# Layer 0's low parts of tiles 4 to 7 as ACT negation plus an adding DMA, ACT's code checks and POOL's bias sums in other places

## The reference

```
# layer 0
e      = leaky_0.2((x * a0) @ x.T)                 # 1024 x 1024, symmetric
alpha  = sigmoid(where(adj == 1, e, -inf))
x1     = layernorm(x + alpha @ x + bias)
# layer 1
H      = x1 @ W ;  s = H @ a_src ;  d = H @ a_dst
E      = where(adj != 0, exp(-leaky_0.2(s_i + d_j)), 0)
out    = layernorm(x1 + elu((E @ H) / rowsum(E)))
```

## Time and profile before

| | |
|---|---|
| median of 3 runs | 1370.85 us (1370.57 to 1371.18) |
| the profiled execution | 1369.6 us |
| its span, first to last instruction | 1367.8 us |
| PE busy | 1275.9 us, 93% |
| DVE, ACT, POOL busy | 1029.2, 856.0, 842.4 us |
| TensorE clock, mean granted | 0.993 |

### The profile page before, as it was taken

The page is one execution under the profiler, slowest core; times in us unless marked ns, Lnnn a source line. Parts: engine busy times, 40 slices in busy tenths (PEclk is TensorE's granted clock), DMA queues, the critical chain, the costliest instruction groups (busy, mean ns, idle before and its releaser), DMA issues.

```text
span 1367.8 us, 27395 instructions
## 1 busy us (share of the span) xinstructions
PE 1275.9 (93%) x7874; PEld 1139.3 (83%) x7874; DVE 1029.2 (75%) x2594; ACT 856.0 (63%) x2130; POOL 842.4 (62%) x1228
## 2 busy tenths in 40 slices
PE   5799999999999999999999999999999998999986
PEld 4788888888888888888888888888888888888875
DVE  5777778787777877778777787877878777787865
ACT  4746757476575756757476575756757567574643
POOL 4746749476583855839466583865839567394732
PEclk9999999999999999999999999999999999999999
DMA  8162350614325162350624415153250623406001
GB/s 173 32 109 74 67 109 19 119 58 87 94 41 102 45 111 73 59 113 12 121 63 73 104 28 110 54 100 80 54 119 16 111 73 65 108 14 124 28 5 34
DMA packets 190352, 101.73 MB, mean 74 GB/s; under 512 B 140656, under 2 KB 173808, under 8 KB 190320
## 3 DMA queue, kind: packets, MB, share of 16 engines
q1 hardware_dynamic: 171888, 67.79, 21.2%
q0 software_dynamic: 18432, 33.56, 14.6%
HBM read 84.55 MB, written 16.78 MB: 74 GB/s over the span
## 4 chain that ended last, share of the span: by engine, by line
PE 39%; POOL 24%; DVE 20%; issue 11%; ACT 5%; DMA 0%; DVEq 0%; POOLq 0%; ACTq 0%
POOL coef_lo L369 13%; PE acc_bank L1227 11%; PE hh_bank L1206 5%; DVE coef L880 5%; PE acc_bank L1108 4%; PE acc_bank L1110 4%; PE acc_bank L1109 4%; PE lg_bank L1108 3%; PE lg_bank L1110 3%; PE lg_bank L1109 3%; POOL var_eps L377 3%; POOL rstd L380 2%; POOL rstd L390 2%; DVE stats L920 2%; DVE reluP L915 2%
## 5 line engine op out<-in xcount | busy, mean ns | idle before, releaser
L1227 PE MATMUL acc_bank<-H,coef 128*128 128x258 f32 x2048 | 469.1, 382 | 10.9 <-ACT reluP L606 9.6
L1227 PEld LDWEIGHTS acc_bank<-H,coef 128*128 128x128 f32 x2048 | 381.7, 190 | 73.7 <-issue 20.2
L369 POOL TENSOR_TENSOR coef_lo<-coef,coef_hi 128x1024 fp32r<-128x1024 f32 x128 | 305.7, 2389 | 62.2 <-ACT coef_hi L552 60.3
L1108 PE MATMUL acc_bank<-h_hi,coef_hi 128*128 128x256 f32 x1024 | 297.4, 290 | 0.0
L1110 PE MATMUL acc_bank<-h_hi,coef_lo 128*128 128x256 f32 x1024 | 286.3, 280 | 0.0
L1109 PE MATMUL acc_bank<-h_lo,coef_hi 128*128 128x256 f32 x1024 | 286.1, 279 | 0.0
L880 DVE SCALAR_TENSOR_TENSOR coef<-tr_bank,E_col,codeT 128x256 f32<-128x256 f32 x512 | 209.1, 476 | 39.3 <-PE acc_bank L1227 36.8
L1108 PEld LDWEIGHTS acc_bank<-h_hi,coef_hi 128*128 128x128 f32 x1024 | 194.8, 190 | 1.0
L1109 PEld LDWEIGHTS acc_bank<-h_lo,coef_hi 128*128 128x128 f32 x1024 | 195.0, 190 | 0.0
L1110 PEld LDWEIGHTS acc_bank<-h_hi,coef_lo 128*128 128x128 f32 x1024 | 194.7, 190 | 0.0
L552 ACT ACTIVATE coef_hi<-coef 128x1024 fp32r<-128x1024 f32 x128 | 135.7, 1060 | 84.6 <-DVE coef L819 84.1
(11 more groups left out here) (77 smaller groups left out, 2283.5 us busy)
## 6 DMA issues: line engine op xcount, KB each, us to landing
code_nat<-in_adj POOLq DMA_DIRECT2D x128, 256.0 KB, 5.3
x_raw<-in_x SPq DMA_DIRECT2D x16, 1024.0 KB, 5.6
out<-x SPq DMA_DIRECT2D x128, 128.0 KB, 1.7
codeT<-code_nat SPq DMA_TRANSPOSE x128, 3.3
W_ext<-in_L_gnn_W SPq DMA_DIRECT2D x1, 256.0 KB, 4.2
eluE<-in_L_gnn_a SPq DMA_DIRECT2D x1, 256.0 KB, 4.6
bias_bc<-in_L_gnn_bias SPq DMA_DIRECT2D x1, 128.0 KB, 4.1
a_col<-in_L_gnn_a SPq DMA_DIRECT2D x4, 1.0 KB, 4.6
```

The source lines that it names most:

```text
L369: nc.gpsimd.tensor_tensor(coef_lo[:, t % 4, :, :], blocks(coef[:, t % 4, :]), f32(coef_hi[:, t % 4, :, :]), ALU.subtract).then_inc(S.lo0, 1)
L1108: nc.tensor.matmul(dst, lhs_hi, rhs_hi, start=first, stop=False)
L1227: ins = nc.tensor.matmul(acc_bank[t % 2][:, 0:HC], coef[:, SLOT1[t], J * P:(J + 1) * P], H[:, J, :], start=J == 0, stop=J == NT - 1)
```

## The change

- For layer 0's tiles 4 to 7 (steps 1 to 4), ACT runs a second activation after `coef_hi`: `coef_lo = -1 * coef`, rounded like `coef_hi`. `hi0` is raised after it. POOL no longer subtracts; it issues a DMA from `coef` to `coef_lo` that adds, and PE and DVE wait on that DMA's semaphore. Tiles 0 to 3 keep POOL's subtraction.
- POOL's `next_bias` comes behind `low0` of the same step.
- ACT's `watch_codes`: tile 0 stays in step 0, tiles 1 to 3 go to steps 5 to 7, tiles 4 to 7 go to the border, one each ahead of chunk 4's scaling, `keep_H(7)`, chunk 6's and chunk 7's scaling.

```diff
             def low0(S, b, t):
                 pool.wait_ge(S.hi0, NT * b + t + 1)
-                nc.gpsimd.tensor_tensor(coef_lo[:, t % 4, :, :], blocks(coef[:, t % 4, :]),
-                                        f32(coef_hi[:, t % 4, :, :]), ALU.subtract).then_inc(S.lo0, 1)
+                if S is F and t >= 4:
+                    pool.sem_inc(pool_past, 1)
+                    pool.dma_start(f32(coef_lo[:, t % 4, :, :]), blocks(coef[:, t % 4, :]),
+                                   accum_op=ALU.add).then_inc(F.lo0_added[t % 4], 16)
+                else:
+                    nc.gpsimd.tensor_tensor(coef_lo[:, t % 4, :, :], blocks(coef[:, t % 4, :]),
+                                            f32(coef_hi[:, t % 4, :, :]), ALU.subtract).then_inc(S.lo0, 1)
...
+                    if 1 <= t and t + 3 < NT:
+                        low0(F, b, t + 3)
                     if nxt and t >= 2:
                         if t == 2:
                             pool.wait_ge(F.x_loaded, 16 * (b + 2))
                         next_bias(b, t - 2)
-                    if 1 <= t and t + 3 < NT:
-                        low0(F, b, t + 3)
...
-                nc.scalar.activation(coef_hi[:, t % 4, :, :], blocks(coef[:, t % 4, :]),
-                                     ACT.Copy).then_inc(S.hi0, 1)
+                ins = nc.scalar.activation(coef_hi[:, t % 4, :, :], blocks(coef[:, t % 4, :]), ACT.Copy)
+                if S is F and t >= 4:
+                    ins = nc.scalar.activation(coef_lo[:, t % 4, :, :], blocks(coef[:, t % 4, :]), ACT.Copy,
+                                               scale=-1.0)
+                ins.then_inc(S.hi0, 1)
...
-                    if t < 6:
+                    if t < 1:
                         watch_codes(b, t)
...
-                    if t in (6, 7):
-                        watch_codes(b, t)
+                    if 5 <= t < 8:
+                        watch_codes(b, t - 4)
                 keep_H(F, b, 6, prev, False)
                 keep_x1T(F, b, 7, prev)
                 if nxt:
                     scale_scores(b + 1, 3)
+                watch_codes(b, 4)
                 if nxt:
                     scale_scores(b + 1, 4)
+                watch_codes(b, 5)
                 keep_H(F, b, 7, prev, False)
                 ends_H(F, b)
                 if nxt:
                     scale_scores(b + 1, 5)
+                watch_codes(b, 6)
                 if nxt:
                     scale_scores(b + 1, 6)
+                watch_codes(b, 7)
                 if nxt:
                     scale_scores(b + 1, 7)
...
             def aggregate0(S, b, t, prev):
-                pe.wait_ge(S.lo0, NT * b + t + 1)
+                if S is GEN:
+                    pe.wait_ge(GEN.lo0, NT * b + t + 1)
+                elif t < 4:
+                    pe.wait_ge(F.lo0, 4 * b + t + 1)
+                else:
+                    pe.wait_ge(F.lo0_added[t % 4], 16 * b + 16)
```

More of the change, by code:

```diff
@@ L66, in __init__ @@
         self.lo0 = sem(tag + "lo0")
+        if not general:
+            self.lo0_added = [sem(tag + f"lo0_added{i}") for i in range(4)]
         self.agg0 = sem(tag + "agg0")
@@ L246, in two_graph_layers @@
         sp_past = sem("sp_past")
+        pool_past = sem("pool_past")
         flag_step = sem("flag_step")
@@ L802, in mask0_below @@
                 if t >= 4:
-                    dve.wait_ge(F.lo0, NT * b + t - 3)
+                    dve.wait_ge(F.lo0, 4 * b + t - 3)
                 elif prev:
@@ L873, in mask1_pair @@
                 elif 2 <= t < 6:
-                    dve.wait_ge(F.lo0, NT * b + t + 4)
+                    for i in range(2):
+                        dve.wait_ge(F.lo0_added[t - 2 + i], 16 * b + 16)
                 elif t == 6:
```

## The result

1394.01 us median (1392.8 to 1396.45) against 1370.71 (1369.95 to 1371.18): 1.0173 times as long, 95% interval 1.0155 to 1.0190. I had forecast 1370 and a range up to 1384, so the kernel is slower than anything the range held.

A forecast was written before the change was run, and what follows sets the result against it. PE, busy 93%, was taken as the bound. A replay of steps 3 to 6 on one graph's clock gave 15 x (1.50 border loss - 1.42 layer 0 saving) - 1.5 = -0.3 us: 1370 us forecast, range 1359 to 1384.

The forecast's parts named there:

- The border term: Border between layers: moved checks make `keep_H(7)`, chunk 7 and all of layer 1 1.50 us later a graph.
- The hidden DMA: Tile 4's adding DMA has 7.57 us before PE wants it; landing in 5.3 to 8, counted as hidden.
- The freed mask: DVE's mask of tile 5, free of POOL's subtraction, takes 1.03 us instead of 2.25.
- the unit cost of the issue: POOL's issue of an adding DMA: 0.57 us, as a code load's, starting 0.08 after ACT's signal.
- step 4: Layer 0, mask of tile 6 behind the moved bias sum: PE waits 0.48 us, before 0.62.
- step 5: Layer 0, mask of tile 7 behind issue and bias sum: PE waits 0.09 us, before 0.55.
- step 3: Layer 0, mask of tile 5 freed from POOL's subtraction: PE's wait falls from 1.58 us to 0.
- the last graph: It has no next graph's bias sums: 2.5 us saved in layer 0, 1.03 lost to checks, together -1.5.
- Step 6: Layer 0: a new PE wait of 0.76 us as the bias sum meets `norm0(4)`; 0.35 without the meeting.
- The faster rival: Layer 0: bias sum and `norm0(4)` don't meet, 1.83 us saved a graph, 1364 us; faster cases' chance 0.29.
- The dear issue: POOL's issue costs more than a code load's; at 1.13 us +17, 1387 us; chance 0.20.
- POOL no freer: The mask holds the square root anyway, so layer 0 gains nothing: 1393 us; chance only part of 0.20.

The follow-up runs named there:

- e1: The kernel before, with only ACT's code checks moved to the changed kernel's places, POOL still subtracting: 1390.86 us, 1.0148 times the kernel before.
- e9: Changed kernel, checks of tiles 4, 5 in steps 7, 8, bias sums of tiles 0 to 2 in the border, tile 4's issue behind `power0(1)`: 1344.36 us.
- e10: The kernel before, POOL subtracting, checks of tiles 1 to 3 in steps 5 to 7, 4 and 5 in steps 7 and 8, 6 and 7 in the border: 1363.67 us.
- e5: The changed kernel with tile 4's check in step 7, tile 5's in step 8, and two in the border behind `keep_H(7)`: 1367.31 us.
- e13: The changed kernel with each adding DMA cut into two of half the size, so POOL issues twice as often: 1426.47 us.
- e3: The changed kernel with each adding DMA issued one step later, behind the next `power0` and ahead of the bias sum: 1395.32 us.

## Why the prediction was wrong

**The border term was right.** Forecast 1.50 us a graph, measured 1.27. ACT reaches `keep_H(7)` at 508.14 without idling, scalings and checks go back to back, and PE pays at `g_col` (0.52) and at chunk 7 (1.13). e1 shows it by itself.

**The hidden DMA was right**: 4.6 us, against the replay's 7.57. **The freed mask was right**: 0.99 for tile 5 against the replay's 1.03. **The masks behind the bias sum** end 1.03 and 1.16 us after it (479.87 against 478.84, 485.40 against 484.24), as the replay had it (1.01 and 1.14).

**The step that failed is the unit cost of the issue.** I took it as a code load's, 0.57, and POOL's answer as the subtraction's, 0.08: 0.65 us from ACT's signal to the issue's end. Measured it is 1.48 to 1.58. Some 0.55 of the excess are the answer (0.63 against 0.08) and some 0.33 the issue itself (0.9 against 0.57). The code loads' row has POOL busy up to them; in such a place, as e9 shows, the first part can't be seen. `norm0` comes 3.78 us behind the end of ACT's negation at step 4 and 3.87 at step 5 (480.33 less 476.55; 485.86 less 481.99), where the replay had 2.83 and 2.96: 0.95 and 0.91 late, of which the issue is 0.88 and 0.84. At step 3 it is 0.87 (474.97 less 472.49 is 2.48; the replay's 467.17 less 465.56 is 1.61). There the square root stands on POOL behind the issue and ends 0.87 after it (474.94 against 474.07). With the counted 0.65 it would have been ready ahead of the replay's `norm0`; with 1.58 it is what `norm0` waits for, so the 0.87 are the issue's too.

The sum with the measured terms, over the 15 graphs ahead of the last: layer 0 was to save 21.3 us and lost 1.9, 23.2 more; the border lost 19.1 instead of 22.5, 3.4 less; the last graph was to bring 1.5 and brought 0.3 (1.4 in layer 0, where PE waits 1.7 us against the 3.1 of the earlier trace rows, less 1.1 at `g_col`), 1.2 more; and PE's own busy time grew by 4.3, which the forecast had at nothing. -0.3 + 23.2 - 3.4 + 1.2 + 4.3 = 25.0, against 24.8 between the two profiled executions. By the last section's count the clock makes 2.2 of the 4.3; the rest is not explained.

**Step 6 fell the other way.** The bias sum and `norm0(4)` did not meet (0.40, and PE waits 0.17), since everything ahead of the bias sum had become later. The faster rival's condition came true and was worth nothing, because the waits had moved to steps 3 to 5.

**The rivals.** The dear issue was the right one: I gave it 0.20 and priced it at +17 for 1.13 us. What came, 1.40 to 1.50 behind an answer of 0.08, lies above that upper bound. With some 0.9 missing, its rule of counting the excess twice gives 0.9 x 2 x 15 = 27, and layer 0 fell short by 23.2. It should have had the larger chance: the only row for an issue was of one with no wait ahead. "POOL no freer" named nearly the right time, 1393, by luck, for a reason that the trace denies: POOL is 99 us freer, and the masks no longer wait for a subtraction.

**What the forecast counted and did not see** is that the checks' leaving layer 0 is a gain by itself (e10, 6 us), larger than what the adding DMA is worth there, which is a loss of 3.6 (e5 less e10) until the bias sums go elsewhere.

## What to carry to other kernels

An instruction that is replaced by a DMA's issue is not gone from its queue. Price the issue from a row where it stands behind a wait on another engine, and list what is queued behind it and which engine's next instruction that will meet. When work is moved off one engine's busy stretch, look for an idle one that no other engine's path runs through (here POOL's in the border, 7.8 us in one piece), and price the place that it is moved to by what waits behind it: two checks of 1.13 us cost 27 us more ahead of `keep_H(7)` and chunk 4's scaling than in steps 7 and 8. A change of several parts needs the control that leaves out each one: what gained by itself, the checks' leaving steps 1 to 4, was hidden behind the loss at the place where they went.

## What the runs showed of the hardware

**The issue behind a wait.** 0.58 to 0.63 us from the signal to the issue's record, and none of it where POOL was busy meanwhile (e9). The issue itself holds POOL for 0.9 us, of 512 KB or of 256 (e13), though the next record starts 0.56 to 0.66 behind its start. That record is longer by about as much as the two overlap: the bias sum has 1.03 behind one issue and 1.36 behind two, and ends 0.75 to 0.78 behind the issue's end each time.

**DVE and POOL.** `norm0` beside a bias sum ends 0.15 to 0.16 us after it, whether that makes it 0.81, 1.35 or 1.72 long, and beside an issue alone it takes 0.41 (e9, and e3's last graph). By the Trainium skill, in "SBUF — State Buffer", section "Who interferes with whom", the shared port goes whole to one of the two; that agrees with the ends of these rows, while two of the three `norm0` here have the earlier start by their records and still end last.

**What a wait of PE costs beside itself.** The windows view of the changed kernel, stretches of 0.5 us (sum, PE busy and its instructions, granted clock, DMA share, GB/s), behind the border's wait of one graph:

```profile
931.00:931.50 0.50, 0.00 (x0) 1.00 0.00 0
931.50:932.00 0.50, 0.27 (x1) 0.84 0.00 0
932.00:932.50 0.50, 0.50 (x3) 0.50 0.67 135
...
934.50:935.00 0.50, 0.50 (x2) 0.50 1.10 202
935.00:935.50 0.50, 0.50 (x3) 0.75 0.47 94
```

PE had waited 0.51 us for `g_col` and 1.13 for `leaky_scores`, and the granted clock went from 2.4 to 1.2 GHz for 3.4 us, 1.7 us lost. Most graphs of the same run have the same waits without it. Added up over windows of 1 us, the clock took 9.4 us before, 11.6 after, 21.8 in e13 and 4.4 in e9. In e13, with waits of 1.1 to 1.7 us ahead of them, there are seven such stretches between 50 and 1300 us. Of the 33.8 us by which e13's span is longer than the changed kernel's, 21.8 - 11.6 = 10.2 are the clock's, beside 19.1 of waits. That the waits bring the low clock on is not shown, as most of them have none behind them; if they do, a wait in e13 cost half as much again as its length.
